# A two-stage transformer block on one core: the last FFN but one moved forward, VectorE steps moved by a slot, transposes released tile by tile

## The chip, the cores and the metric

The kernel runs on one core of one Trainium2 chip. TensorE (PE in the rows) multiplies and transposes, VectorE (DVE), ScalarE (ACT) and GpSimd (POOL) do the elementwise work, and SyncE's queue (SPq) issues the transfers. The metric is the device time of one execution in microseconds (us). The kernel before was timed three times and profiled once more.

## The reference

Sixteen sequences of 512 tokens with 256 features go through four residual steps. `a` is attention with 16 heads of 64, `b` is attention with 16 heads of 16 and rotary positions.

```python
x = x + attn_a(layernorm(x))      # returns X + gelu(A) @ Wpost, 16 heads of 64
x = x + ffn(layernorm(x))         # relu(x @ W1q.T + b1) @ W2q.T + b2, W1q and W2q of -1, 0, 1
x = x + attn_b(layernorm(x))      # rotary on q and k, 16 heads of 16, biases
x = x + ffn(layernorm(x))         # the same weights again
```

## The kernel before

The program is one list of slots per engine. Stage one (slots up to 540 or so) does attention `a` for all sequences and is not touched. Stage two starts 554 slots later (`SHIFT`) and does everything else. In stage two a slot is one unit of attention `b`: 32 units for each sequence, so that slots 32w to 32w+31 belong to sequence w. They are called **window w** here. A slot has two **steps**, and step r of window w is written r; slot k of a window holds steps 2k and 2k+1.

In each slot TensorE computes the scores of one unit (`scores`, L724), which VectorE reduces to their maximum (`unit_max`, L1160). From slot 11 of window 0 on, the scores of every unit go into the same PSUM banks, so the scores of slot k+1 wait for the maximum of slot k. TensorE then computes the turned scores of a unit 11 slots back (`turned_scores`, L738), which ScalarE exponentiates (`exps`, L867), and in every second slot the products with the values (`values`, L751). What TensorE does beside this is set by a table of steps for each sequence s, counted from step 64s. In steady state these fall into window w:

* first FFN of sequence w+2 ("ffn0"): transposes of the normalised tokens (`XT0`, steps 38 and 39 of the window), eight "up" products (`UP0`, steps 44 to 53), four "down" products (`DOWN0`, from step 56 on),
* q, k and v of sequence w+1 (`QK`, `VB`), their rotation on GpSimd (`ROTATE`), and the split into high and low parts: the high part on ScalarE (`parts_high`, L937, table `HIGHS`), the low part on VectorE (`parts_low`, L1154, table `LOWS`, steps 36, 38, 44 and 46 of the window),
* output projection ("wo", L767, `WO1`) and second FFN ("ffn1") of sequence w-1, whose `WO1` begins at step 34; the down products end in window w+1.

A layer norm is five VectorE or ScalarE pieces at the steps in `NORM`: statistics of two tiles (L1122), statistics of the other two, `aggregate` (L1128 to L1131), and twice two tiles normalised into the one buffer `xn` (L1136 on VectorE for ffn1, L875 on ScalarE for the others). The inverse deviation, a power over 4 columns, is GpSimd's (`inverse_deviation`, L554) and stands one step behind `aggregate` in GpSimd's own list. At the same place in that list stand the low parts of the hidden features (`hidden_low`, L569, three steps behind their "up"), and the addition of a bias to the four tiles at once (`add_bias`, L563, step 40 of the window for ffn0). After each transpose ScalarE makes the high part `xh` one step later and VectorE the low part `xl` two steps later (L1219). The high part of the first hidden tile (`hidden_high`, L919) waits until all low parts of the rotated q and k (L1154) are made, since they share memory. Every engine works through its list in order, and a wait holds back all that stands behind it.

Each engine's loop fixes the order inside one step. For VectorE it is:

```python
for todo in steps_of.get(step - 1, []): empty(*todo)
for todo in steps_of.get(step - 2, []): empty_low(*todo)
...
if step % 2 == 0 and 0 <= step // 2 < UNITS_ALL: unit_max(step // 2)
...
for piece, part, s in norm_steps.get(step, []): ...   # statistics, aggregate, normalise
... invert_sums, scale_heads, parts_low
```

For GpSimd `hidden_low` of step - 3 stands ahead of `inverse_deviation` of step - 1, and that ahead of `add_bias`.

The buffer `x_before` holds the tokens of one sequence from its output projection to the end of its second FFN. It is loaded at step 93 (`load_before`, L441), after the save of the sequence before (`save_before`, L446) has landed.

Of the kernel before, what the change touches and what calls it, by code (L numbers as in the profile page):

```python
# [13 lines left out]
def hybrid_block_kernel(nc, X, WQ, WK, WV, WPOST, WB, BQK, BV, WO, BO, W1T, B1, W2T, B2, COS, SIN, X1, M1, OUT):  # L14
# [6 lines left out]
    BATCH, S, D = X.shape  # L21
    TB = S // P
    KT = D // P
# [6 lines left out]
    FT = FF // P  # L30
# [9 lines left out]
    with ctx:  # L40
# [51 lines left out]
        wo = at("wo", 30, [P, QUADS // 2, D])  # L92
# [78 lines left out]
        xn_ready = sem("xn_ready")  # L171
# [65 lines left out]
        def bank(fill):  # L237
            return banks[fill % 3]
# [67 lines left out]
        QK, VB = (-41.5, -40, -38, -36), (-34, -33.5, -31.6, -31.1)  # L306
        WO1, XT1 = (98.5, 100.5, 104.5, 106.5), (118.1, 119.1)
        UP1, DOWN1 = (128, 129, 130.5, 132, 133, 134.5, 136.5, 138.5), (140.5, 142.5, 146.5, 148.5)
        NORM = {"ffn0": (-101, -100, -98, -93, -91), "attn": (-67, -64, -63, -51, -49), "ffn1": (103, 108, 109, 113, 115)}
        UP_RAMP, DOWN_RAMP, XTB_RAMP = tuple(range(-66, -58)), (-57, -55.5, -54, -52.5), (-45.9, -44.9)  # L310
        ATTN_RAMP = (-54, -51, -50, -48, -47)
        BIAS = {"ffn0": -88, "attn": -45, "ffn1": 124}
        ROTATE, HIGHS, LOWS = (-39, -37, -35, -34, -32, -30), (-31, -29, -23, -21), (-28, -26, -20, -18)
        STACK = (-17, -15, -11, -9, 5, 7, 21, 23)
        INVERT, SCALE_HEADS = (41, 57, 73, 90), (46, 62, 76, 92)
        SLOT = 2 * UNITS
# [2 lines left out]
        plan = []  # L319
        for s in range(BATCH):  # L320
            plan += [(XT0[k], "transpose", "ffn0", k, s) for k in range(KT)]
            plan += [((UP_RAMP if s == 1 else UP0)[f], "up", "ffn0", f, s) for f in range(FT)]
            plan += [((DOWN_RAMP if s == 1 else DOWN0)[t], "down", "ffn0", t, s) for t in range(TB)]
            plan += [((XTB_RAMP if s == 1 else XTB)[k], "transpose", "attn", k, s) for k in range(KT)]
            plan += [(QK[j], "qk", "attn", j, s) for j in range(4)]
            plan += [(VB[t], "v", "attn", t, s) for t in range(TB)]
            plan += [(WO1[t], "wo", "ffn1", t, s) for t in range(TB)]
            plan += [(XT1[k], "transpose", "ffn1", k, s) for k in range(KT)]
            plan += [(UP1[f], "up", "ffn1", f, s) for f in range(FT)]
            plan += [(DOWN1[t], "down", "ffn1", t, s) for t in range(TB)]  # L330
        plan = sorted((SLOT * s + at_step, kind, part, i, s) for at_step, kind, part, i, s in plan)

        at_of = {}
# [18 lines left out]
                    steps_of.setdefault(step, []).append((kind, part, i, s, fill))  # L352

        def norm_at(part, s):
            return ATTN_RAMP if (part, s) == ("attn", 1) else NORM[part]

        norms = sorted((SLOT * s + norm_at(part, s)[0], part, s) for s in range(BATCH) for part in NORM)
        nth_norm = {(part, s): n for n, (_, part, s) in enumerate(norms)}
# [31 lines left out]
        with nc.Block() as block:  # L390
            @block.sync
            def _(sp):
# [101 lines left out]
                for slot in range(FIRST_A, LAST + SHIFT):  # L494
# [15 lines left out]
                    for step in (2 * (slot - SHIFT), 2 * (slot - SHIFT) + 1):  # L510
                        for s in range(BATCH):
# [10 lines left out]
                                max_rows(s, (r - 12) // 8)  # L522
                            if r == 93:
                                load_before(s)
                            if r == 152:
                                save_before(s)
                sp.wait_ge(x_out, 16 * BATCH)

# [1 line left out]
            def _(pool):  # L530
# [64 lines left out]
                for slot in range(FIRST_A, LAST + SHIFT):  # L595
# [13 lines left out]
                    for step in (2 * (slot - SHIFT), 2 * (slot - SHIFT) + 1):  # L609
# [8 lines left out]
                        for s in range(BATCH):  # L618
                            r = step - SLOT * s
                            for part in NORM:  # L620
                                if r == BIAS[part]:
                                    add_bias(part, s)
                            if r in ROTATE and (s or r < ROTATE[3]):
                                rotate(ROTATE.index(r), s)

            @block.tensor
            def _(pe):
# [127 lines left out]
                def product(kind, part, i, s, fill):  # L755
# [10 lines left out]
                        for g in range(QUADS // 2):  # L766
                            last = mm(half, heads_b[:, g, tokens], wo[:, g, :], start=(g == 0), stop=(g == QUADS // 2 - 1))  # L767
                    elif kind == "transpose":
                        pe.wait_ge(xn_ready, TB * (nth_norm[part, s] + 1))
                        for t in range(TB):  # L770
                            last = nc.tensor.transpose(bank(fill)[:, t * P:(t + 1) * P], xn[:, t, i * P:(i + 1) * P], ident[:, :])
                    elif kind == "up":
                        if part == "ffn0" and s == 0:
# [558 lines left out]
```

## Time and profile before

| | before |
|---|---|
| median of 3 runs | 3782.32 us |
| lowest and highest | 3780.09 and 3784.66 us |
| the profiled execution's own time | 3781.21 us |
| its span in the profile | 3779.0 us |
| busy: PE, DVE, ACT, POOL | 3626.6, 2584.8, 2385.9, 1888.6 us |
| granted TensorE clock over the span | 0.986 of full speed |

Stage two begins at about 2248 us of the span. A number in the rows such as `[1.09 <-DVE max_b L1160]` is idle time of the engine just before the instruction, and what ended it. Neighbouring instructions of an engine are pipelined, so that one may start shortly before the end of the last. All times in the rows are from the start of the span.

### The profile page before, as it was taken

The page shows a single profiled execution, that of the slowest core. Times are in us where ns is not written, and L with a number is a line of the kernel's source. Part 1 is how long each engine was busy: PE and PEld are TensorE (multiplying, and loading weights), DVE is VectorE, ACT ScalarE, POOL GpSimd, SP SyncE. Part 2 cuts the span into 40 slices and gives each one's busy share as a digit, 9 for nine tenths or more (in the row PEclk, how much of TensorE's full clock was granted, in tenths as well). Part 3 has the DMA queues.
Part 4 walks back from the last instruction along what each step waited for, and adds up shares of the span by engine and source line. Part 5 has one row for each costly group of instructions (what it writes and reads, how often), then busy time and mean ns, then how long its engine had stood idle before and what let it go on. Part 6 is the DMA issues. An engine that isn't in the chain of part 4 may idle for free.

```text
span 3779.0 us, 64440 instructions
## 1 busy us (share of the span) xinstructions
PE 3626.6 (96%) x23810; PEld 2433.1 (64%) x23810; DVE 2584.8 (68%) x4296; ACT 2385.9 (63%) x4629; POOL 1888.6 (50%) x1337
## 2 busy tenths in 40 slices
PE   8999999999999999999999978999999999999987
PEld 6777777777777777777777664555555555555534
DVE  6766666666667666666767656777777777777763
ACT  5665656556566566655656546777777777777754
POOL 4555555556555555555654633444444444444412
PEclk9999999999999999999999998999999999999989
DMA  2000000000000000000000012222222222222220
GB/s 79 7 12 1 12 12 12 1 12 12 1 12 12 1 12 12 9 5 12 12 1 15 25 43 47 53 62 62 63 62 61 61 63 58 62 59 64 53 48 18
DMA packets 102329, 116.27 MB, mean 31 GB/s; under 512 B 23557, under 2 KB 75269, under 8 KB 102021
## 3 DMA queue, kind: packets, MB, share of 16 engines
q1 hardware_dynamic: 102020, 112.17, 12.0%
q8 instruction: 193, 3.16, 0.4%
q14 instruction: 116, 0.94, 0.1%
HBM read 34.48 MB, written 27.26 MB: 16 GB/s over the span
## 4 chain that ended last, share of the span: by engine, by line
PE 76%; DVE 11%; ACT 7%; issue 5%; POOL 1%; DMA 0%; DVEq 0%; ACTq 0%; SPq 0%
PE ps_o L675 12%; PE ps_s L644 10%; PE ps_t L657 8%; PE ps_t L226 8%; PE ps_m L657 4%; PE ps_o L751 4%; PE ps_t L233 4%; DVE max_b L1160 4%; PE ps_t L786 4%; PE ps_m L226 3%; PE ps_t L710 3%; PE ps_s L724 3%; ACT et L867 2%; PE ps_m L233 2%; PE ps_s L738 2%
## 5 line engine op out<-in xcount | busy, mean ns | idle before, releaser
L534 POOL TENSOR_TENSOR e_a<-e_a,recip 128x1024 f32<-128x1024 f32 x512 | 969.4, 1894 | 948.7 <-DVE recip L1027 948.5
L825 ACT ACTIVATE e_a<-ps_s,neg_max 128x512 f32<-128x512 f32 x1024 | 695.1, 685 | 544.8 <-DVE neg_max L1020 544.4
L1160 DVE TENSOR_REDUCE max_b<-ps_s 128x2 f32<-128x1024 f32 x512 | 625.0, 1221 | 270.6 <-PE ps_s L724 268.8
L867 ACT ACTIVATE et<-ps_s 128x1024 f32<-128x1024 f32 x512 | 527.4, 1030 | 319.9 <-PE ps_s L738 319.0
L1020 DVE TENSOR_REDUCE neg_max<-ps_s 128x2 f32<-128x1024 f32 x512 | 623.0, 1217 | 67.7 <-PE ps_s L644 67.7
L675 PE MATMUL ps_o<-et_a,v_a 128*64 128x256 f32 x4096 | 499.8, 386 | 9.1 <-DVE heads_a L1063 4.8
L644 PE MATMUL ps_s<-raw_a 64*128 64x512 f32 x3072 | 425.9, 409 | 5.5 <-ACT e_a L825 5.3
L675 PEld LDWEIGHTS ps_o<-et_a,v_a 128*64 128x64 f32 x4096 | 279.2, 137 | 192.1 <-issue 78.3
L657 PE MATMUL ps_t<-ident,e_a 128*128 128x128 f32 x2660 | 394.0, 280 | 2.1 <-DVE xl L1219 2.0
L1034 DVE COPY et_a<-ps_t 128x512 f32<-128x512 f32 x366 | 251.1, 688 | 206.3 <-PE ps_t L657 202.1
L657 PEld LDWEIGHTS ps_t<-ident,e_a 128*128 128x128 f32 x2660 | 290.1, 141 | 133.2 <-issue 129.3
L569 POOL TENSOR_TENSOR h_lo<-h,h_hi 128x512 fp32r<-128x512 f32 x215 | 276.1, 1290 | 179.6 <-ACT h_hi L919 177.5
L644 PEld LDWEIGHTS ps_s<-raw_a 64*128 64x128 f32 x3072 | 270.2, 184 | 129.2 <-issue 74.2
L724 PE MATMUL ps_s<-k_stack,q_stack 48*128 48x512 f32 x1024 | 261.0, 506 | 64.1 <-DVE max_b L1160 61.4
L751 PE MATMUL ps_o<-et,v_b 128*32 128x512 f32 x2048 | 283.0, 625 | 0.0
L573 POOL TENSOR_TENSOR m_parts<-max_b,m_parts 128x8 fp32r<-128x8 f32 x128 | 28.2, 221 | 481.6 <-ACT m_parts L909 481.6
L832 ACT ACTIVATE et_a<-ps_t 128x512 f32<-128x512 f32 x299 | 178.4, 597 | 115.7 <-PE ps_t L657 115.7
L724 PEld LDWEIGHTS ps_s<-k_stack,q_stack 48*128 48x128 f32 x1024 | 97.7, 186 | 233.2 <-DVE max_b L1160 107.8
L738 PE MATMUL ps_s<-q_stack,k_stack 50*128 50x512 f32 x1024 | 214.0, 412 | 11.1 <-ACT et L867 10.4
L657 PE MATMUL ps_m<-ident,e_a 128*128 128x128 f32 x1436 | 224.6, 279 | 0.0
L1045 DVE SCALAR_TENSOR_TENSOR raw_a<-ps_t,raw_a 128x512 fp32r<-128x512 f32 x181 | 124.3, 687 | 129.9 <-ACT raw_a L851 124.8
L825 ACT ACTIVATION_READ_ACCUMULATOR e_a<-ps_s,neg_max 128x1 f32 x1024 | 202.8, 198 | 0.0
(194 smaller groups left out, 7231.0 us busy)
## 6 DMA issues: line engine op xcount, KB each, us to landing
q_stack<-roped_q SPq DMA_DIRECT2D x256, 96.0 KB
k_stack<-roped_k SPq DMA_DIRECT2D x256, 96.0 KB
x_a<-X SPq DMA_DIRECT2D x16, 512.0 KB, 3.4
X<-x_a SPq DMA_DIRECT2D x16, 512.0 KB, 2.9
x_ahead<-X SPq DMA_DIRECT2D x16, 512.0 KB, 3.8
X<-x_ahead SPq DMA_DIRECT2D x16, 512.0 KB, 2.9
x_before<-X SPq DMA_DIRECT2D x16, 512.0 KB, 3.9
OUT<-x_before SPq DMA_DIRECT2D x16, 512.0 KB, 5.2
```

Source lines behind the costliest of these rows:

```text
L226: last = nc.tensor.matmul(out, w[:, k, c0:c0 + P], xs[:, k, :], start=(i == 0), stop=(i == len(todo) - 1))
L534: nc.gpsimd.tensor_tensor(e_a[:, u % 5, :, :], e_a[:, u % 5, :, :], factor, ALU.mult).then_inc(e_normed, 1)
L644: last = mm(ps_s[:, 2 * j + h, :], raw[rows, q_part, c:c + P], raw[rows, k_part, :], start=(m == 0), stop=(m == 2))
L657: last = nc.tensor.transpose(bank(fill)[:, c:c + P], e_a[:, u % 5, j, t * P:(t + 1) * P], ident[:, :])
L675: last = mm(out, v_a[:, t, c:c + HA], et_a[:, 2 * (q % 2):2 * (q % 2) + 2, t, h, :], start=(t == 0), stop=(t == TB - 1))
L724: last = mm(ps_s[:, score_bank(u) + h, :], q_stack[rows, pair, block_ * P:(block_ + 1) * P], k_stack[rows, pair, :], start=True, stop=True)
L738: last = mm(ps_s[:, 2 + h, :], k_stack[rows, pair, keys * P:(keys + 1) * P], q_stack[rows, pair, :], start=True, stop=True)
L751: last = mm(ps_o[32 * h:32 * (h + 1), :], v_b[:, s % 2, keys, 4 * quad + h, :], et[:, (2 * w + h // 2) % 5, h % 2, :], start=(keys == 0), ...
L825: ins = nc.scalar.activation(e_a[:, u % 5, h, :], ps_s[:, 2 * (u % 2) + h, :], ACT.Exp, bias=neg_max[:, u % 5, h:h + 1], accum_out=sums[:, ...
L867: nc.scalar.activation(et[:, v % 5, :, :], ps_s[:, 2:4, :], ACT.Exp)\
L1020: nc.vector.reduce_max(neg_max[:, u % 5, :], ps_s[:, 2 * (u % 2):2 * (u % 2) + 2, :], AX.X, negate=True)\
L1160: nc.vector.reduce_max(max_b[:, u // 4 % 2, :, u % 4], ps_s[:, score_bank(u):score_bank(u) + 2, :], AX.X, negate=True).then_inc(max_done, 1)
```

## The change

Four parts.

1. For sequence 14 alone, the output projection, the transposes, the up and the down products, the norm, the bias and the save get earlier steps (`WO_EARLY` and so on): wo from step 34.5 of window 15 to 31.5, the up products from 64 to 46.1, the down products from 76.5 to 57.5 and the save from 88 to 66. Slots 21 to 31 of the last window have neither ffn0 nor q, k and v products, since no sequences follow.
2. In every window the second low part of q moves from step 38 to 40 (`LOWS`).
3. For every other sequence the ffn1 statistics move from steps 39 and 44 of the window to 43 and 45, and `aggregate` from 45 to 46.
4. In stage two the first transposes of a norm wait for their token tiles one by one and not for all four.

```diff
-        NORM = {..., "ffn1": (103, 108, 109, 113, 115)}
+        NORM = {..., "ffn1": (107, 109, 110, 113, 115)}
+        WO_EARLY, XT_EARLY, FFN_EARLY = (95.5, 96.5, 98.5, 99.5), (107.1, 108.1), (99, 101, 102, 104, 105)
+        UP_EARLY, DOWN_EARLY = (110.1, 111, 112, 113.5, 115, 116.5, 118, 119), (121.5, 123.5, 125.5, 127)
+        BIAS_EARLY, SAVE_EARLY = 107, 130
...
-        ROTATE, HIGHS, LOWS = (-39, -37, -35, -34, -32, -30), (-31, -29, -23, -21), (-28, -26, -20, -18)
+        ROTATE, HIGHS, LOWS = (-39, -37, -35, -34, -32, -30), (-31, -29, -23, -21), (-28, -24, -20, -18)
...
-            plan += [(WO1[t], "wo", "ffn1", t, s) for t in range(TB)]
-            plan += [(XT1[k], "transpose", "ffn1", k, s) for k in range(KT)]
-            plan += [(UP1[f], "up", "ffn1", f, s) for f in range(FT)]
-            plan += [(DOWN1[t], "down", "ffn1", t, s) for t in range(TB)]
+            early = s == BATCH - 2
+            plan += [((WO_EARLY if early else WO1)[t], "wo", "ffn1", t, s) for t in range(TB)]
+            plan += [((XT_EARLY if early else XT1)[k], "transpose", "ffn1", k, s) for k in range(KT)]
+            plan += [((UP_EARLY if early else UP1)[f], "up", "ffn1", f, s) for f in range(FT)]
+            plan += [((DOWN_EARLY if early else DOWN1)[t], "down", "ffn1", t, s) for t in range(TB)]
...
+            return FFN_EARLY if (part, s) == ("ffn1", BATCH - 2) else NORM[part]
...
-                            if r == 152:
+                            if r == (SAVE_EARLY if s == BATCH - 2 else 152):
                                 save_before(s)
...
-                                if r == BIAS[part]:
+                                if r == (BIAS_EARLY if (part, s) == ("ffn1", BATCH - 2) else BIAS[part]):
                                     add_bias(part, s)
...
                     elif kind == "transpose":
-                        pe.wait_ge(xn_ready, TB * (nth_norm[part, s] + 1))
                         for t in range(TB):
+                            if i == 0:
+                                pe.wait_ge(xn_ready, TB * nth_norm[part, s] + t + 1)
                             last = nc.tensor.transpose(...)
```

**VectorE, window 10, slots 19 to 21.** This is the piece from the maximum of slot 19 to that of slot 21, first before. `roped_q` is the low part of q, `token_rows` and `recip_b` are the inversion of the softmax sums.

```order
L1160 TENSOR_REDUCE max_b<-ps_s 128x2
L1154 TENSOR_TENSOR roped_q<-q_rot,roped_q 128x512
L1122 BN_STATS stats<-x_before 128x6 x2
L1219 TENSOR_TENSOR xl<-ps_t,xh 128x512
L1160 TENSOR_REDUCE max_b<-ps_s 128x2
L1219 TENSOR_TENSOR xl<-ps_m,xh 128x512
L1199 STREAM_TRANSPOSE token_rows<-weighted 128x512
L1201 RECIPROCAL recip_b<-token_rows 128x16
L1160 TENSOR_REDUCE max_b<-ps_s 128x2
```

The same piece in the changed kernel:

```order
L1167 TENSOR_REDUCE max_b<-ps_s 128x2
L1226 TENSOR_TENSOR xl<-ps_t,xh 128x512
L1167 TENSOR_REDUCE max_b<-ps_s 128x2
L1161 TENSOR_TENSOR roped_q<-q_rot,roped_q 128x512
L1226 TENSOR_TENSOR xl<-ps_m,xh 128x512
L1206 STREAM_TRANSPOSE token_rows<-weighted 128x512
L1208 RECIPROCAL recip_b<-token_rows 128x16
L1167 TENSOR_REDUCE max_b<-ps_s 128x2
```

The low part has moved from ahead of the maximum of slot 20 to behind it, and the statistics have left the piece; they come behind the maximum of slot 21.

**GpSimd, a window of the steady state, from the ffn0 bias on.** `rstd` is the power, `h_lo` the low parts of the hidden tiles. Before:

```order
L573 TENSOR_TENSOR m_parts<-max_b,m_parts 128x8
L563 TENSOR_TENSOR x_ahead<-x_ahead,b_rows 128x1024
L554 TENSOR_TENSOR rstd<-rstd,minus_half 128x4
L569 TENSOR_TENSOR h_lo<-h_107,h_hi 128x512 x2
L573 TENSOR_TENSOR m_parts<-max_b,m_parts 128x8
L569 TENSOR_TENSOR h_lo<-h_107,h_hi 128x512 x5
```

In the changed kernel:

```order
L569 TENSOR_TENSOR x_ahead<-x_ahead,b_rows 128x1024
L575 TENSOR_TENSOR h_lo<-h_107,h_hi 128x512
L560 TENSOR_TENSOR rstd<-rstd,minus_half 128x4
L575 TENSOR_TENSOR h_lo<-h_107,h_hi 128x512
L579 TENSOR_TENSOR m_parts<-max_b,m_parts 128x8
L575 TENSOR_TENSOR h_lo<-h_107,h_hi 128x512 x5
```

The power now stands behind the first low part of the hidden tiles. This is so in windows 1 to 13, where a ffn1 norm and the up products of ffn0 meet.

**TensorE, window 15, slots 23 to 25.** Before, the three slots hold the attention's own products alone:

```order
L724 MATMUL ps_s<-k_stack,q_stack 128x512 x2
L738 MATMUL ps_s<-q_stack,k_stack 128x512 x2
L751 MATMUL ps_o<-et,v_b 32x512 x4
L724 MATMUL ps_s<-k_stack,q_stack 128x512 x2
L738 MATMUL ps_s<-q_stack,k_stack 128x512 x2
```

In the changed kernel, the same place up to the scores of slot 24:

```order
L730 MATMUL ps_s<-k_stack,q_stack 128x512 x2
L744 MATMUL ps_s<-q_stack,k_stack 128x512 x2
L757 MATMUL ps_o<-et,v_b 32x512 x4
L784 MATMUL ps_t<-xh,w_80 128x512 x2
L784 MATMUL ps_t<-xl,w_80 128x512 x2
L784 MATMUL ps_m<-xh,w_80 128x512 x2
L784 MATMUL ps_m<-xl,w_80 128x512 x2
L730 MATMUL ps_s<-k_stack,q_stack 128x512 x2
```

Two up products of sequence 14 have come between the values of slot 23 and the scores of slot 24.

## Rows read from the trace of the kernel before

**Rows 1.** Waits of TensorE over the whole span: total us, times, longest.

```profile
PE ps_s L724 <- DVE max_b L1160: 61.4, 90, 1.5
...
PE ps_m L771 <- ACT xn L875: 10.1, 2, 6.4
```

**Rows 2.** Timeline of VectorE: the maximum of slot 19 in windows 8 and 9.

```profile
3035.56 1.21 DVE L1160 TENSOR_REDUCE max_b<-ps_s 128x2 f32<-128x1024 f32 x1
...
3127.96 1.21 DVE L1160 TENSOR_REDUCE max_b<-ps_s 128x2 f32<-128x1024 f32 x1
```

**Rows 3.** Timeline of VectorE in window 10, slots 18 to 25 (start, us).

```profile
3220.17 1.21 DVE L1154 TENSOR_TENSOR roped_q<-q_rot,roped_q 128x512 fp32r<-128x512 f32 x1
...
3221.90 1.21 DVE L1160 TENSOR_REDUCE max_b<-ps_s 128x2 f32<-128x1024 f32 x1
...
3224.30 0.67 DVE L1219 TENSOR_TENSOR xl<-ps_t,xh 128x512 fp32r<-128x512 f32 x1
3224.89 1.21 DVE L1160 TENSOR_REDUCE max_b<-ps_s 128x2 f32<-128x1024 f32 x1
3226.02 0.68 DVE L1219 TENSOR_TENSOR xl<-ps_m,xh 128x512 fp32r<-128x512 f32 x1
...
3227.64 1.23 DVE L1160 TENSOR_REDUCE max_b<-ps_s 128x2 f32<-128x1024 f32 x1
...
3234.06 0.69 DVE L1154 TENSOR_TENSOR roped_k<-k_rot,roped_k 128x512 fp32r<-128x512 f32 x1
...
3236.09 2.21 DVE L1136 TENSOR_SCALAR xn<-x_before,mean_var,rstd 128x256 f32<-128x256 f32 x2
3238.22 1.21 DVE L1160 TENSOR_REDUCE max_b<-ps_s 128x2 f32<-128x1024 f32 x1
```

**Rows 4.** Timeline of TensorE in window 10: the scores of slots 21, 22 and 26.

```profile
3226.15 0.50 PE L724 MATMUL ps_s<-k_stack,q_stack 48*128 48x512 f32 x2 [1.09 <-DVE max_b L1160]
...
3228.92 0.50 PE L724 MATMUL ps_s<-k_stack,q_stack 48*128 48x512 f32 x2
...
3240.19 0.50 PE L724 MATMUL ps_s<-k_stack,q_stack 48*128 48x512 f32 x2
```

**Rows 5.** Timeline of GpSimd in window 10, slots 17 to 25.

```profile
3218.32 2.51 POOL L587 TENSOR_TENSOR k_rot<-k_rot 128x512 f32<-128x512 f32 x2
...
3224.58 2.37 POOL L563 TENSOR_TENSOR x_ahead<-x_ahead,b_rows 128x1024 f32<-128x1024 f32 x1
3232.77 1.02 POOL L554 TENSOR_TENSOR rstd<-rstd,minus_half 128x4 f32<-128x4 f32 x1 [5.83 <-DVE rstd L1131]
3235.55 2.59 POOL L569 TENSOR_TENSOR h_lo<-h,h_hi 128x512 fp32r<-128x512 f32 x2 [1.77 <-ACT h_hi L919]
```

**Rows 6.** Timeline of ScalarE in window 10: the first hidden tile's high part.

```profile
3234.84 0.63 ACT L919 ACTIVATE h_hi<-h 128x512 fp32r<-128x512 f32 x1 [1.43 <-DVE roped_k L1154]
```

**Rows 7.** Timeline of VectorE in window 15: the maximum of slots 0 and 11.

```profile
3625.04 1.23 DVE L1160 TENSOR_REDUCE max_b<-ps_s 128x2 f32<-128x1024 f32 x1 [0.72 <-PE ps_s L724]
...
3658.70 1.22 DVE L1160 TENSOR_REDUCE max_b<-ps_s 128x2 f32<-128x1024 f32 x1
```

**Rows 8.** Timeline of TensorE: the first two output projections of the last sequence.

```profile
3739.68 3.42 PE L767 MATMUL ps_m<-wo,heads_b 128*128 128x256 f32 x8 [3.05 <-DVE heads_b L1213]
```

**Rows 9.** Timeline of SyncE's queue: the load of sequence 14's `x_before`.

```profile
3670.09 0.38 SPq L441 DMA_DIRECT2D x_before<-X  x1
```

**Rows 10.** Timeline of ScalarE: exponentials of turned scores behind the last scores.

```profile
3704.35 1.02 ACT L867 ACTIVATE et<-ps_s 128x1024 f32<-128x1024 f32 x1 [0.65 <-PE ps_s L738]
...
3705.97 1.03 ACT L867 ACTIVATE et<-ps_s 128x1024 f32<-128x1024 f32 x1 [0.39 <-PE ps_s L738]
...
3733.57 1.03 ACT L867 ACTIVATE et<-ps_s 128x1024 f32<-128x1024 f32 x1 [2.50 <-PE ps_s L738]
```

**Rows 11.** Timeline of VectorE: residual of the last output projection.

```profile
3744.57 0.69 DVE L1186 TENSOR_TENSOR x_before<-x_before,ps_m 128x512 f32<-128x512 f32 x1 [5.04 <-DMA x_before<-X]
```

**Rows 12.** Busy time in a stretch of window 15: PE, PEld, DVE, ACT, POOL, granted clock.

```profile
3668.00:3675.00 7.00, 5.87 (x20) 2.35 (x20) 2.67 (x4) 2.26 (x3) 0.20 (x1) 0.52 0.31 87
```

More of the change, by code:

```diff
@@ L308, in hybrid_block_kernel @@
         UP1, DOWN1 = (128, 129, 130.5, 132, 133, 134.5, 136.5, 138.5), (140.5, 142.5, 146.5, 148.5)
-        NORM = {"ffn0": (-101, -100, -98, -93, -91), "attn": (-67, -64, -63, -51, -49), "ffn1": (103, 108, 109, 113, 115)}
+        NORM = {"ffn0": (-101, -100, -98, -93, -91), "attn": (-67, -64, -63, -51, -49), "ffn1": (107, 109, 110, 113, 115)}
+        WO_EARLY, XT_EARLY, FFN_EARLY = (95.5, 96.5, 98.5, 99.5), (107.1, 108.1), (99, 101, 102, 104, 105)
+        UP_EARLY, DOWN_EARLY = (110.1, 111, 112, 113.5, 115, 116.5, 118, 119), (121.5, 123.5, 125.5, 127)
+        BIAS_EARLY, SAVE_EARLY = 107, 130
         UP_RAMP, DOWN_RAMP, XTB_RAMP = tuple(range(-66, -58)), (-57, -55.5, -54, -52.5), (-45.9, -44.9)
@@ L354, in norm_at @@
         def norm_at(part, s):
-            return ATTN_RAMP if (part, s) == ("attn", 1) else NORM[part]
+            if (part, s) == ("attn", 1):
+                return ATTN_RAMP
+            return FFN_EARLY if (part, s) == ("ffn1", BATCH - 2) else NORM[part]
         norms = sorted((SLOT * s + norm_at(part, s)[0], part, s) for s in range(BATCH) for part in NORM)
```

## Prediction

> **What bounds the kernel now.** I read the table of busy time first, then TensorE's waits, then the timeline of one window of the steady state, and the end last. TensorE is busy for 3626.6 of 3779.0 us, so what counts is any time in which it waits, and any wait that is added. Its largest wait is for the running maximum on VectorE: 61.4 us in 90 places [rows 1]. The windows repeat: the maximum of slot 19 comes 92.40 us after that of the window before (3035.56 to 3127.96), and 93.94 us in the next one (3221.90) [rows 2, 3]. The second figure matters: in that window something held the engines up for 1.5 us, and the windows after it run 1.5 us later. A delay of TensorE inside a window is carried to the end in full, and the same holds for a gain. I take window 10 as the pattern.
>
> There the scores of slot 21 wait 1.09 us for the maximum of slot 20 [rows 4]. VectorE was late with it: between the maxima of slots 19 and 20 (3221.90 and 3224.89) stand the second low part of q, the statistics and `xl` [rows 3]. The change takes the first two out of this place. That is its gain, and it can be at most 1.09 us in a window.
>
> **Parts 2 and 3, where the moved instructions come to stand (windows 1 to 13).** Step by step, in the times of window 10:
>
> (a) Between the two maxima only `xl` is left. It began at 3224.30 behind the others and now begins when ScalarE's part is there, at about 3223.3, so the maximum of slot 20 starts near 3224.0 instead of 3224.89 and ends near 3225.2. The scores of slot 21 come 0.9 us earlier.
>
> (b) The low part of q now starts at 3225.2. GpSimd is then in its bias addition, from 3224.58 to 3226.95 [rows 5]. What that does is seen one slot earlier in the same trace: the first low part of q starts at 3220.17 while GpSimd works until 3220.83 (3218.32 + 2.51) and takes 1.21 us, ending 0.55 us after GpSimd, where a low part without such a neighbour takes 0.69 [rows 3, 5]. `xl`, which reads PSUM, takes 0.68 beside the bias addition, undisturbed [rows 3, 5]. So the low part ends at 3226.95 + 0.55 = 3227.5. Behind it stand `xl`, the transposition and the reciprocal, 1.62 us as before (3226.02 to 3227.64) [rows 3]. The maximum of slot 21 starts at 3229.0 instead of 3227.64, and the scores of slot 22 at 3230.3 instead of 3228.92 [rows 4]: the gain has become a loss of 1.4 us.
>
> The Trainium skill says of this place (SBUF — State Buffer, section Who interferes with whom) that a VectorE instruction with two SBUF inputs and a GpSimd instruction that reads SBUF exclude each other for the whole of the one that came first. By that rule as written the low part would run its full 0.69 us after GpSimd and not 0.55, and 13 windows would cost 1.8 us more than the sum below.
>
> (c) The statistics and `aggregate` now stand in slots 21 to 23, so VectorE is behind with each maximum. Adding the spacings of its instructions, the maximum of slot 22 starts at 3231.8, of slot 23 at 3234.3, and the last low part of k, in slot 23, ends at 3237.0 instead of 3234.75 (3234.06 + 0.69) [rows 3]. ScalarE's high part of the first hidden tile waits for just that: it starts at 3237.1 instead of 3234.84 [rows 6].
>
> (d) GpSimd now makes the low part of that tile before the power. It can start at 3237.8 (0.71 us behind the high part, as in rows 5 and 6), takes 1.3 us, and the power 1.02 [rows 5]: the inverse deviation is there at 3240.1, where before it was there at 3233.8. VectorE's `xn` stands behind the maximum of slot 24, which ends at 3238.2, and waits for it with the maximum of slot 25 queued behind. The two tiles of `xn` took 2.21 us beside GpSimd's low parts [rows 3, 5]; between 1.7 (one GpSimd instruction in the way) and 3.0 us (two) are possible now. The maximum of slot 25 then starts between 3241.8 and 3243.1 instead of 3238.22, and the scores of slot 26 between 3243.1 and 3244.4 instead of 3240.19 [rows 3, 4]. That is 2.9 to 4.2 us a window. I take 3.5, near the middle, because nothing tells which of the two it will be. Slots 26 to 31 are bound by TensorE and hide nothing.
>
> Thirteen windows: 13 x 3.5 = +45.5 us (37.7 to 54.6). Window 0 has (b) without statistics: +1 (0 to 1.4). Window 14 has no bias addition and no ffn0 products: 0.
>
> **Part 1, the last window.** The slots without added products are set by VectorE: the maximum, then 0.6 us until the next scores are there, about 1.9 us a slot. Slots 0 to 10 of the window, with the same up and down products of sequence 13, took 33.66 us for 11 slots [rows 7]. The early FFN puts these products into slots 23 to 31, nine slots. I take off the one empty slot (1.8 us) and the attention of another (1.2), and get 30.7 us. The transfer into `x_before` is issued at 3670.09 [rows 9] and lands about 4 us later, but the first residual now stands in VectorE's list at slot 16, about 3670; VectorE waits there until 3674, and the norm's pieces fall into VectorE-bound slots, so slot 23 begins some 2.3 us later than before. Slot 31 then ends near 3718.5. Behind it eleven turned scores are left, at 1.62 us each, as between 3704.35 and 3705.97, where before they took 27.6 us for ten beside the FFN [rows 10]. The last exponential starts at 3735 by this and 3733.57 before [rows 10]; with TensorE at half clock for part of it, as it fell after sparse slots in the granted clock of 0.52 from 3668 to 3675 [rows 12], 3735 to 3739. Then two gains: no down product of sequence 14 stands ahead of the last values (-0.9), and the last residual, which waited 5.04 us for its transfer until 3744.57 [rows 11], waits for its own products only (-1.3, as they end at 3743.1 [rows 8]). Together +1 us, between -1.5 and +4. So what the change was to remove from behind the last scores comes back in front of them, almost to the microsecond.
>
> **Part 4.** The last token tile arrives when it did, and only three transposes move ahead of it, some 0.5 us at each place where TensorE waits for `xn`: two at the ramp, where it waits 10.1 us in all [rows 1], and one at the end. -1.5 us (0 to -2). In the steady state TensorE doesn't wait there: 0.
>
> **Sum.** +45.5 + 1 + 1 - 1.5 = +46 us against the profiled execution's 3781.2, so 3827.2; the median of the runs is 1.1 above it: 3828 us. Its own range, from the bounds, is 3814 to 3843.
>
> **The rivals.**
>
> *Half of it: GpSimd does not hold the low part up.* Then (b) costs nothing, slot 22 is 0.3 us early, but (d) remains, since it hangs on the order in GpSimd's list: the power at 3238.4, the scores of slot 26 at 3242.0, +1.8 us a window, 13 x 1.8 = 23, so 3805 us. Against it speaks the 1.21 us of the first low part; for it that no row shows this very pair. 0.17.
>
> *Faster.* The bias addition and the reversed order fall into idle time, and the wait at slot 21 disappears: 13 x 1.09 = -14, and -1 at the ends: 3767 us. It needs the power done before the maximum of slot 24 has ended (3238.2), that is, a first hidden tile whose high part starts by 3235.2, as it did before (3234.84). With VectorE late by (c) it does not. 0.07.
>
> *No change.* The gain at slot 21 and the later waits cancel because ScalarE, relieved by the delay, catches up for the rest of the window: 3782 us. The 1.5 us that were carried on in full speak against it. 0.05.
>
> *The last window costs much more.* As forecast, and the dense slots 23 to 31 are bound by ScalarE (an exponential and two hidden-tile instructions for each up product), then the turned scores run at half clock throughout: +11 instead of +1, 3838 us. 0.09.
>
> **How the numbers follow.** The forecast has 0.62. A measurement of this kernel can tell about 0.2% from no change, 7.6 us. Faster is the one rival, 0.07; same is no change, 0.05; slower is the rest, 0.88. The range takes in the forecast's own, the last rival and most of the first: 3795 to 3845 us.
>
> **What the changed profile would show.** TensorE's wait of 1.09 us at slot 21 gone or small, and new ones at slots 22 and 26, released by the maximum. The second low part of q at 2.3 us instead of 0.7, ending half a microsecond behind the bias addition. On VectorE an idle time before `xn`, released by the power, in 13 windows. The distance of the windows 95 to 96.5 us instead of 92.4. No wait for the transfer at the end, and one for it near slot 16 of window 15. I would be wrong if the distance stays at 92.4 or falls: then (c) and (d) hide, and the step to look at is the time of the power. If the distance is right and the sum is not, the last window is mis-sized.

## The result, and the profile after

The changed kernel takes 3830.91 us (median of four runs, 3825.96 to 3833.61) and the kernel before, in four runs beside it, 3783.49: a ratio of 1.0124 (95% interval 1.0106 to 1.0141), slower by 47.4 us. The profiled execution has a span of 3830.2 us. The busy times of the engines, two groups of VectorE's, and four of TensorE's waits (total us, times, longest):

```profile
PE 3651.6 (95%) x23810; PEld 2443.5 (64%) x23810; DVE 2618.1 (68%) x4296; ACT 2387.1 (62%) x4629; POOL 1893.0 (49%) x1337
```

```profile
L1161 DVE TENSOR_TENSOR roped_q<-q_rot,roped_q 128x512 fp32r<-128x512 f32 x32 | 54.6, 1708 | 0.0
...
L1143 DVE TENSOR_SCALAR xn<-x_before,mean_var,rstd 128x256 f32<-128x256 f32 x64 | 51.1, 841 | 24.7 <-POOL rstd L560 24.7
```

```profile
PE ps_s L730 <- DVE max_b L1167: 80.8, 87, 2.8
...
PE ps_s L744 <- ACT et L874: 16.0, 27, 1.2
...
PE ps_m L778 <- ACT xn L882: 7.1, 2, 5.0
...
PE ps_t L778 <- DVE xn L1143: 4.5, 1, 4.5
```

The second fence gives, per group, busy time and mean of one in ns. The 32 low parts of q take 54.6 us instead of 29.4, and the longest wait for a maximum is 2.8 us where it was 1.5 [rows 1]. VectorE waits 24.7 us for the power, in front of `xn`.

**Where the time arose.** The two profiled spans differ by 51.2 us. I measured a window by the distance of its maximum of slot 19 to the next one's. It was 92.40 us [rows 2]. Of windows 2 to 13, four now have 94.4 (window 13, whose successor has fewer products, 93.83 where it had 91.80), five have 95.1 to 95.6 and three 96.6 to 96.7. Window 4 begins and ends with these rows of VectorE:

```profile
2677.21 1.21 DVE L1167 TENSOR_REDUCE max_b<-ps_s 128x2 f32<-128x1024 f32 x1
...
2772.77 1.21 DVE L1167 TENSOR_REDUCE max_b<-ps_s 128x2 f32<-128x1024 f32 x1
```

The first maximum of window 15 was at 3625.04 [rows 7] and is at 3666.30, 41.3 us later. Counted from the first maximum of a window to that of the next, 38.5 us of it come from windows 1 to 13, 2.3 from window 0 and 0.5 from before and behind them. The last window and the end add 10 us.

**Window 3, the plain case.** VectorE, from the maximum of slot 19 to that of slot 25:

```profile
2582.84 1.21 DVE L1167 TENSOR_REDUCE max_b<-ps_s 128x2 f32<-128x1024 f32 x1
2584.20 0.69 DVE L1226 TENSOR_TENSOR xl<-ps_t,xh 128x512 fp32r<-128x512 f32 x1 [0.15 <-ACT xh L896]
2584.81 1.22 DVE L1167 TENSOR_REDUCE max_b<-ps_s 128x2 f32<-128x1024 f32 x1
2585.94 2.46 DVE L1161 TENSOR_TENSOR roped_q<-q_rot,roped_q 128x512 fp32r<-128x512 f32 x1
...
2589.94 1.23 DVE L1167 TENSOR_REDUCE max_b<-ps_s 128x2 f32<-128x1024 f32 x1
...
2596.83 0.68 DVE L1161 TENSOR_TENSOR roped_k<-k_rot,roped_k 128x512 fp32r<-128x512 f32 x1
...
2600.62 1.70 DVE L1143 TENSOR_SCALAR xn<-x_before,mean_var,rstd 128x256 f32<-128x256 f32 x2 [1.97 <-POOL rstd L560]
2602.24 1.21 DVE L1167 TENSOR_REDUCE max_b<-ps_s 128x2 f32<-128x1024 f32 x1
```

GpSimd in the same window:

```profile
2585.48 2.38 POOL L569 TENSOR_TENSOR x_ahead<-x_ahead,b_rows 128x1024 f32<-128x1024 f32 x1
2598.32 1.29 POOL L575 TENSOR_TENSOR h_lo<-h,h_hi 128x512 fp32r<-128x512 f32 x1 [10.46 <-ACT h_hi L926]
2599.57 1.02 POOL L560 TENSOR_TENSOR rstd<-rstd,minus_half 128x4 f32<-128x4 f32 x1
```

The second low part of q starts at 2585.94, inside GpSimd's bias addition, and ends at 2588.40, 0.54 us after the addition (2585.48 + 2.38 = 2587.86). Behind it the maximum of slot 21 is late. TensorE's four waits between slots 19 and 31 of this window are these:

```profile
2584.20 0.50 PE L730 MATMUL ps_s<-k_stack,q_stack 48*128 48x512 f32 x2 [0.22 <-DVE max_b L1167]
...
2591.22 0.50 PE L730 MATMUL ps_s<-k_stack,q_stack 48*128 48x512 f32 x2 [2.35 <-DVE max_b L1167]
...
2600.40 0.49 PE L744 MATMUL ps_s<-q_stack,k_stack 50*128 50x512 f32 x2 [0.45 <-ACT et L874]
...
2603.51 0.50 PE L730 MATMUL ps_s<-k_stack,q_stack 48*128 48x512 f32 x2 [0.49 <-DVE max_b L1167]
```

They sum to 3.51 us. Before, window 10 has three, for the scores of slots 20, 21 and 29:

```profile
3223.26 0.50 PE L724 MATMUL ps_s<-k_stack,q_stack 48*128 48x512 f32 x2 [0.19 <-DVE max_b L1160]
...
3248.92 0.50 PE L724 MATMUL ps_s<-k_stack,q_stack 48*128 48x512 f32 x2 [0.51 <-DVE max_b L1160]
```

With the 1.09 at slot 21 [rows 4] that is 1.79. The difference, 1.72, accounts for nearly all of the 1.97 by which the windows lie further apart. This bookkeeping (what TensorE waits, summed over a window) served for the experiments below, where it meets the distance within 0.3 us.

**Window 4, with the clock.** Here the same wait is followed by something that window 3 doesn't have:

```profile
2685.62 0.80 PE L730 MATMUL ps_s<-k_stack,q_stack 48*128 48x512 f32 x2 [2.37 <-DVE max_b L1167]
...
2686.77 1.22 PE L784 MATMUL ps_t<-xh,w 128*128 128x512 f32 x2
...
2691.47 0.73 PE L784 MATMUL ps_t<-xh,w 128*128 128x512 f32 x2
```

```profile
2681.20:2685.50 4.30, 2.05 (x12) 0.76 (x12) 4.23 (x6) 2.15 (x3) 1.05 (x1) 1.00 0.00 0
2685.60:2689.00 3.40, 3.38 (x9) 2.32 (x10) 3.40 (x8) 1.14 (x2) 0.00 (x0) 0.51 0.05 10
```

The columns of the second fence are the stretch, its length, the busy time of PE, PEld, DVE, ACT and POOL, the granted clock, and the share and rate of the DMA. From 2685.6 to 2689.0 TensorE is granted 0.51, its lower level of 1.2 GHz, after a stretch in which it was busy for 2.05 of 4.3 us. In window 3 it was busy for 2.07 us of the same stretch, and the clock did not fall. The up products that take 0.73 us at 2691.47 take 1.22 at 2686.77. Nine of windows 1 to 13 have such a stretch behind the wait at slot 22, and each costs 1.2 us (95.56 from 2677.21 to 2772.77, against 94.37 in window 3).

The kernel before has exactly one, in window 9, and it is the 1.5 us that the prediction had noticed and left at "something held the engines up". TensorE and the stretch, in the kernel before:

```profile
3132.21 0.60 PE L724 MATMUL ps_s<-k_stack,q_stack 48*128 48x512 f32 x2 [1.10 <-DVE max_b L1160]
...
3133.17 1.93 PE L751 MATMUL ps_o<-et,v_b 128*32 128x512 f32 x8
```

```profile
3132.50:3135.90 3.40, 3.40 (x14) 0.99 (x13) 2.47 (x5) 1.97 (x2) 0.47 (x1) 0.50 0.00 0
```

Eight value products take 1.93 us there, and 1.07 at full clock, behind a wait of 1.10 us for the maximum of slot 20.

### The profile page after: what moved, and what is told of

It is laid out like the page before. It is cut to its first block, busy times and chain, and to the rows that moved or that the text cites. A ratio compares the mean times of both kernels' runs of the same rounds, so it can differ in the third digit from the quotient of the medians.

```text
span 3830.2 us, 64392 instructions
## 1 busy us (share of the span) xinstructions
PE 3651.6 (95%) x23810; PEld 2443.5 (64%) x23810; DVE 2618.1 (68%) x4296; ACT 2387.1 (62%) x4629; POOL 1893.0 (49%) x1337
## 4 chain that ended last, share of the span: by engine, by line
PE 79%; DVE 10%; ACT 4%; issue 4%; POOL 1%; DMA 0%; SPq 0%; DVEq 0%; ACTq 0%
PE ps_o L681 12%; PE ps_s L650 10%; PE ps_t L663 8%; PE ps_t L226 8%; PE ps_o L757 5%; PE ps_m L663 4%; PE ps_t L793 4%; PE ps_s L730 4%; PE ps_t L233 4%; PE ps_m L226 3%; PE ps_t L716 3%; DVE max_b L1167 3%; PE ps_s L744 2%; PE ps_t L784 2%; PE ps_m L233 2%
```

## The experiments

I held that GpSimd's bias addition holds the low part up and that this is most of the loss; the rivals were the reversed order of the power and the first low hidden part, the later statistics as such, and the early FFN. Each of the four parts was first made alone on the kernel before; then single steps were put back in the changed kernel. "Distance" is that of the windows, from the profile.

**Part 2 alone.**

```diff
-        ROTATE, HIGHS, LOWS = (-39, -37, -35, -34, -32, -30), (-31, -29, -23, -21), (-28, -26, -20, -18)
+        ROTATE, HIGHS, LOWS = (-39, -37, -35, -34, -32, -30), (-31, -29, -23, -21), (-28, -24, -20, -18)
```

> The kernel before with part 2 alone: the second low part of q at step 40 instead of 38, the statistics where they were. Theory (the low part is held up by GpSimd's bias addition): it takes 2.3 to 2.5 us instead of 0.68, the scores of slot 22 come 1.4 us later, and the windows are 93.8 us apart instead of 92.4; 14 windows make about +20 us, 3803 us, more where the TensorE clock falls behind the new wait. Rival (the low part costs nothing at its new place, only the wait at slot 21 shrinks): windows 91.8 to 92.4 us apart, 3775 to 3783 us.

Measured: 3813.95 us against 3786.80, ratio 1.0074 (1.0057 to 1.0090). VectorE and GpSimd in window 5 of this kernel:

```profile
2776.23 2.05 DVE L1154 TENSOR_TENSOR roped_q<-q_rot,roped_q 128x512 fp32r<-128x512 f32 x1
```

```profile
2775.36 2.38 POOL L563 TENSOR_TENSOR x_ahead<-x_ahead,b_rows 128x1024 f32<-128x1024 f32 x1
```

The low part starts 0.41 us later behind the maximum of slot 19 than in the changed kernel, since the statistics still stand ahead of it, takes 2.05 us instead of 2.46 and ends at the same place, 0.54 us behind the addition. The distance is 93.6 in the four of windows 1 to 13 without a stretch at the lower clock and 94.7 to 94.9 in the nine that have one (94.18 in window 13). TensorE's waits in window 5 sum to 2.94, +1.15 against before; the distance is 1.17 longer. More than half of the whole loss is this one step on the list: 27 us, where 20 were expected, since 13 x 1.17 is 15 us and the stretches at the lower clock add some 11.

**Part 3 alone.**

```diff
-        NORM = {..., "ffn1": (103, 108, 109, 113, 115)}
+        NORM = {..., "ffn1": (107, 109, 110, 113, 115)}
```

> The kernel before with part 3 alone: ffn1 statistics and aggregate at steps 43, 45 and 46. Theory (the power behind the first low part of the hidden tiles in GpSimd's list holds up the normalisation and the maximum of slot 25): slot 22 0.5 us earlier, slot 26 1.0 to 2.3 us later, windows 93.4 to 94.7 us apart, 13 windows make +13 to +30 us, about 3803 us. Rival (only the low part costs): windows 91.9 us apart or less, 3775 us.

Measured: 3786.41 against 3786.80, ratio 1.0004 (0.9995 to 1.0013), distance 92.53, no stretch at the lower clock. The time is that of the kernel before, against an expected 3803 us. The power is late as forecast, and `xn` waits for it:

```profile
2778.87 1.69 DVE L1136 TENSOR_SCALAR xn<-x_before,mean_var,rstd 128x256 f32<-128x256 f32 x2 [1.97 <-POOL rstd L554]
```

```profile
2778.65 0.51 PE L738 MATMUL ps_s<-q_stack,k_stack 50*128 50x512 f32 x2 [0.63 <-ACT et L867]
...
2781.75 0.50 PE L724 MATMUL ps_s<-k_stack,q_stack 48*128 48x512 f32 x2 [0.47 <-DVE max_b L1160]
```

The maximum of slot 25 comes 17.57 us after that of slot 19 (2762.91 in this window) instead of 16.32 [rows 3], and that of slot 28 at 25.89 instead of 25.75. TensorE waits 1.77 us in the window, as before (1.79): 0.64 less at slot 21, nothing at slot 29, and 1.10 more at slots 25 and 26. VectorE's late maximum was paid for out of waits that were there anyway.

**Part 1 alone,** the `_EARLY` tables.

> The kernel before with part 1 alone: the second FFN of sequence 14 early. The profile of the changed kernel puts window 15 and what follows at +10 us, where the forecast had +1. Theory (part 1 costs this by itself): windows 0 to 14 as before, maxima of slots 0 to 31 of window 15 94 us apart instead of 79, the turned scores behind them at half clock, 3791 to 3794 us. Rival (the 10 us come from the other parts or from the late state in which window 15 begins): 3781 to 3785 us.

Measured: 3791.54 against 3786.80, ratio 1.0014 (1.0004 to 1.0023). Distances as before. From the first maximum of window 15 to the end it takes 160.7 us instead of 154.0, +6.7. In three pieces: first to last maximum 91.8 us instead of 79.1 (+12.7); last maximum to last exponential 24.2 instead of 29.5 (-5.3); from there to the end 44.7 instead of 45.4 (-0.8). So the second piece doesn't give back what the first costs. In it TensorE has only the turned scores. The stretch in this kernel:

```profile
3729.00:3750.00 21.00, 14.18 (x56) 3.00 (x54) 2.75 (x6) 9.39 (x10) 0.00 (x0) 0.53 0.08 25
```

It is busy for 14.18 of 21 us and granted 0.53. In the kernel before, the FFN of sequence 14 filled this place:

```profile
3704.00:3722.00 18.00, 16.66 (x87) 8.11 (x84) 3.75 (x7) 16.30 (x25) 8.93 (x8) 1.00 0.01 3
```

There TensorE was busy for 16.66 of 18 us, at full clock. The other profiles say the same. In all six kernels with part 1 (this one, the changed one and four further down) a stretch of 20 to 27 us at the lower clock begins behind the last scores; in the seven without it there is none longer than 4 us up to the last exponential.

**Part 4 alone.**

```diff
-                        pe.wait_ge(xn_ready, TB * (nth_norm[part, s] + 1))
                         for t in range(TB):
+                            if i == 0:
+                                pe.wait_ge(xn_ready, TB * nth_norm[part, s] + t + 1)
```

> The kernel before with part 4 alone: transposes released tile by tile. Theory: windows 1 to 14 unchanged at 92.4 us, TensorE's waits for the normalised tokens shorter by some 0.5 us at each of three places, -1.5 us in all, 3782 us, which the times can't tell from no change. Rival (single waits cost TensorE's queue time at each of the 48 transposes): windows longer by 0.2 us or more.

Measured: 3780.98 against 3786.80, ratio 0.9986 (0.9976 to 0.9995). The waits of TensorE for `xn`, 10.1 us [rows 1] and 5.7 before, are smaller:

```profile
PE ps_m L772 <- ACT xn L876: 7.1, 2, 5.0
...
PE ps_t L772 <- DVE xn L1137: 4.0, 1, 4.0
```

It is the one part of the change that shows a gain by itself.

**The power ahead of the low hidden part,** in the changed kernel.

```diff
+                        for piece, part, s in norm_steps.get(step - 1, []):
+                            if piece == 2:
+                                inverse_deviation(part, s)
...
-                        for piece, part, s in norm_steps.get(step - 1, []):
-                            if piece == 2:
-                                inverse_deviation(part, s)
```

> The changed kernel with GpSimd's list mended: the power stands ahead of the low parts of the hidden tiles again. Theory (low part held up by the bias addition costs most, the power's place adds 0.8 us a window): the low part still takes 2.46 us, windows without a fall of the clock 93.6 to 94.0 us apart instead of 94.4, with a fall 1.2 us more, in all 8 to 12 us less than the changed kernel, about 3821 us. Rival (the power's place is the main cost): windows 92.4 us apart, 3792 us.

Measured: 3829.72 against 3786.86, ratio 1.0103 (1.0088 to 1.0118). In window 4 of this kernel the power no longer stands behind a low hidden part, and `xn` doesn't wait:

```profile
2691.94 1.12 POOL L560 TENSOR_TENSOR rstd<-rstd,minus_half 128x4 f32<-128x4 f32 x1 [10.01 <-DVE rstd L1138]
```

```profile
2694.01 2.32 DVE L1143 TENSOR_SCALAR xn<-x_before,mean_var,rstd 128x256 f32<-128x256 f32 x2
```

Yet `xn` takes 2.32 us instead of 1.69 (two low hidden parts run beside it from 2693.59 on), and the distance falls by 0.14 us alone (94.23 without, 95.43 with a stretch at the lower clock), where at least 0.4 were expected. The three windows of 96.7 us are gone, but twelve of windows 1 to 13 have a stretch at the lower clock instead of nine, which takes most of that back: about 1 us less in all than the changed kernel, where 8 to 12 were expected. In a plain window, a step that VectorE waited 2 us for was worth next to nothing.

**The bias one step earlier,** in the changed kernel: GpSimd's addition then begins 0.4 us before the maximum of slot 19 and not 2.6 us behind it.

```diff
-        BIAS = {"ffn0": -88, "attn": -45, "ffn1": 124}
+        BIAS = {"ffn0": -89, "attn": -45, "ffn1": 124}
```

> The changed kernel with the ffn0 bias addition one step earlier in GpSimd's list, so that it starts about 3 us earlier and is over when the second low part of q comes. Theory: that low part takes 0.68 us again, the wait at slot 22 shrinks below 0.6 us, the clock doesn't fall in windows 2 to 13, windows 92.6 to 93.2 us apart, 3795 to 3800 us, of which 7 to 10 us are the early FFN's. Rival (the low part is long at its new place for another reason): 2.46 us and windows 94.4 to 96.7 us apart as in the changed kernel.

Measured: 3791.27 against 3786.86, ratio 1.0014 (1.0004 to 1.0023). Window 5:

```profile
2761.46 0.68 DVE L1161 TENSOR_TENSOR roped_q<-q_rot,roped_q 128x512 fp32r<-128x512 f32 x1
```

```profile
2757.89 2.37 POOL L569 TENSOR_TENSOR x_ahead<-x_ahead,b_rows 128x1024 f32<-128x1024 f32 x1 [0.65 <-ACT xn L882]
```

The addition ends at 2760.26, the low part starts at 2761.46 and takes 0.68. The distance is 92.6, no window has a stretch at the lower clock, and TensorE's waits sum to 1.70. One number in the table of biases takes away 43 of the 47 us, some 4 more than expected.

**Both.**

> The changed kernel with both mended, bias addition and power first. Theory: windows 92.1 to 92.4 us apart, the scores of slot 22 0.3 us earlier than before, and what is left is the early FFN: 3788 to 3792 us. Rival (statistics so late cost by themselves, since VectorE is behind from slot 21 to 24): windows 92.8 us or more.

Measured: 3787.09 against 3786.86, ratio 1.0000 (0.9990 to 1.0009); distance 92.45, just above the expected 92.1 to 92.4, and so not the 92.8 of the rival.

**Both, without part 1.**

> As the run with both mended, without the early FFN (parts 2, 3 and 4 with the bias addition and the power first). Theory: windows 92.1 to 92.4 us apart and the end of the kernel before, 3777 to 3783 us, the lowest time of all. Rival (as for the run with both mended): windows 92.8 us or more, 3787 us.

Measured: 3784.42 against 3786.86, ratio 0.9991 (0.9981 to 1.0000). The windows are as forecast, 92.45 us apart, but the time is not the lowest of all: 3777 to 3783 us were expected. The two medians differ by 2.7 us and their intervals overlap, so these runs don't show that the early FFN costs anything in this setting. The profiled execution, the slowest of the ten, takes 160.0 us from the first maximum of window 15 to the end, 6 more than the kernel before, although the FFN of sequence 14 is at its old place. The lower clock lies ahead of the last scores there:

```profile
3691.50:3715.20 23.70, 20.11 (x76) 7.23 (x75) 15.08 (x24) 10.75 (x14) 4.01 (x5) 0.50 0.02 3
```

The profile with part 2 alone has the same from 3715.5 to 3739.4. So the last window can be slow without part 1 too, and why it was in these two is open.

**The hold-up in the kernel before.** Only the bias moves, by one step; nothing of the change is made. The addition now lies on the low part's old place.

```diff
-        BIAS = {"ffn0": -88, "attn": -45, "ffn1": 124}
+        BIAS = {"ffn0": -89, "attn": -45, "ffn1": 124}
```

> The kernel before with one edit that the change does not have: the ffn0 bias addition one step earlier in GpSimd's list, so that it falls on the second low part of q at its old place. Theory (a VectorE instruction with two SBUF inputs waits for GpSimd's): that low part starts 1.13 us and the bias addition 0.4 us before to the maximum of slot 19, runs until 0.55 us behind the end of the addition and takes 1.3 us instead of 0.68; the maximum of slot 20 comes 0.6 us later and the windows are 93.0 us apart, 3788 to 3792 us. Rival (the long low part is a matter of its place in VectorE's list): 0.68 us and 92.4 us.

Measured: 3810.88 against 3784.86, ratio 1.0075 (1.0062 to 1.0087).

```profile
2768.43 2.38 POOL L563 TENSOR_TENSOR x_ahead<-x_ahead,b_rows 128x1024 f32<-128x1024 f32 x1 [0.62 <-ACT xn L875]
```

```profile
2770.01 1.33 DVE L1154 TENSOR_TENSOR roped_q<-q_rot,roped_q 128x512 fp32r<-128x512 f32 x1
```

The addition ends at 2770.81, the low part at 2771.34, 0.53 us behind it. Held up by 0.65 us, it makes the maximum of slot 20 late by 0.66 (3.65 us behind that of slot 19, before 2.99). The distance is 93.07 in the plain windows, +0.67, and 93.9 to 97.0 in the nine with stretches at the lower clock. The hold-up is as forecast and makes 9 of the 26 us; the time, 20 us above the forecast, is not, for the lower clock was left out of it. The same edit that mends the changed kernel spoils the one before.

**The changed kernel without part 2.**

> The changed kernel with part 2 alone undone (the second low part of q back at step 38). Theory (part 2 is what costs, through the hold-up by GpSimd, and brings the falls of the clock with it): windows 92.5 us apart, no fall of the clock in windows 2 to 13, and of the loss only the early FFN's 5 to 8 us left: 3788 to 3792 us. Rival (the four parts cost only together, or the late statistics do): 3805 us or more.

Measured: 3791.53 against 3784.86, ratio 1.0017 (1.0008 to 1.0026), distance 92.52, no stretch at the lower clock. So part 2 costs most of it and part 3 hardly anything without it. Together they cost more than apart, 1.97 us in a plain window against 1.17 and 0.13. The low part ends with GpSimd's addition in either case, so the maximum of slot 21 starts 7.10 us behind that of slot 19, with part 3 or without it. This is the maximum of slot 21 in window 5 with part 2 alone, where that of slot 19 starts at 2772.72:

```profile
2779.82 1.23 DVE L1160 TENSOR_REDUCE max_b<-ps_s 128x2 f32<-128x1024 f32 x1
```

What part 3 saves at slot 21 is lost in that hold-up, and the waits at slots 25 and 26 that it brings come on top.

**A milder early FFN with part 4, on the kernel before.** The up products begin at slot 26 of the last window, the first ones two slots apart, and the down products stay behind the last scores.

```diff
+        WO_EARLY, XT_EARLY, FFN_EARLY = (98.5, 100.5, 102.5, 104.5), (111.1, 112.1), (103, 105, 106, 108, 110)
+        UP_EARLY, DOWN_EARLY = (116, 120, 124, 128, 129, 130.5, 132.5, 134.5), (136.5, 138.5, 140.5, 142.5)
+        BIAS_EARLY, SAVE_EARLY = 121, 146
```

> The kernel before with part 4, and a milder early FFN for sequence 14: three up products in slots 26, 28 and 30 of the last window, which have no products with the values and so a wait of TensorE of about 1 us each, the rest behind the scores, down products and save three slots earlier than before. Theory (dense slots cost what they save, free ones don't): the last 31 maxima 79 to 81 us apart, turned scores behind them 3 to 4 us shorter, no wait for the transfer at the end, -3 to -6 us in all, 3776 to 3780 us. Rival (the clock takes it back: sparser turned scores at half clock): within 2 us of the kernel before.

Measured: 3779.87 against 3784.86, ratio 0.9991 (0.9982 to 1.0000). From the first maximum of window 15 to the end it takes 150.7 us, before 154.0 and with part 4 alone 151.4, and TensorE stays at full clock behind the last scores:

```profile
3708.00:3726.00 18.00, 16.01 (x94) 9.25 (x90) 3.10 (x8) 12.89 (x20) 6.57 (x6) 1.00 0.01 2
```

So spreading the FFN avoids the loss, but the gain over part 4 alone, 0.6 us in the profiles, is below what the runs can tell. Part 4 by itself is the best that I can name.

## Why the prediction was right, and where it was not

The forecast was 3828 us, and 3831 was measured. The mechanism was right for the first half of the window; the sum came out because wrong terms cancelled: the 13 windows' waits were priced 20 us too high (45.5 for 25.6), stretches at the lower clock and a late `xn` in three windows, 14 us, were not in the sum, and the last window was 9 us too low. The range from its own bounds was also added up wrongly at the lower end: the terms give 3816 to 3842, not 3814 to 3843.

**Step (a), right.** `xl` alone stands between the maxima, and the second of them starts 1.97 us after the first; the forecast had 2.1 (3224.0 against 3221.90). TensorE's wait at slot 21 is gone.

**Step (b), right.** In times after the maximum of slot 19, forecast and then measured: low part's end 5.6 and 5.56, maximum of slot 21 7.1 and 7.10, scores of slot 22 8.4 and 8.38. The bias one step earlier took all of it away, and the same hold-up appeared in the kernel before when the addition was moved onto its low part, so the cause is shown by runs in both directions. The Trainium skill (SBUF — State Buffer, Who interferes with whom) says that the pair of ports that the two share is an exclusive lock, and that the one that comes second blocks fully. The pairing that it names, a VectorE instruction with two SBUF inputs against GpSimd's, is the one seen. That the blocked one then needs its whole time doesn't hold here: it ends 0.53 to 0.54 us after GpSimd in three kernels, and alone it takes 0.68.

**Step (c), right within 0.4 us.** The maximum of slot 22 starts at 9.60 (forecast 9.9), that of slot 23 at 11.98 (12.4), and the first hidden tile's low part at 15.48 (15.9).

**Step (d), the one that failed.** "The maximum of slot 25 then starts between 3241.8 and 3243.1", that is 19.9 to 21.2 after slot 19; it was 19.40. `xn` took 1.69 us, my lower bound, where I had taken the middle. More important is the next sentence, "Slots 26 to 31 are bound by TensorE and hide nothing". The scores of slot 26 come at 20.67 instead of 18.29, +2.38 and not +3.5, and 0.4 of that is gone by slot 29, where TensorE had waited 0.51 us for a maximum before and no longer does. I had that row within reach and did not look past slot 26. So of the 3.5 us, 0.65 were `xn`, 0.4 the lateness carried over from (c), and 0.4 what slot 29 gives back. Of the 2.38 us at slot 26, 1.36 were there at slot 22 already (8.38 instead of 7.02), by (b) alone. The two runs on this step agree: late statistics alone cost 0.13 us a window, since the waits that go at slots 21 and 29 pay for the late maximum of slot 25, and the order of the power is worth 0.14. In the plain windows the loss is 1.97 us, not 3.5. The rival "half of it", 1.8 us a window, named almost this price, but for the opposite reason: it kept (d) and dropped (b), and the runs keep (b) and all but drop (d).

**What was not forecast.** TensorE's clock falls in nine of thirteen windows after the wait at slot 22, 1.2 us each, 11 us together. Three windows have a further 1.1 us, at slot 26, where the second pair of `xn` runs beside GpSimd longer:

```profile
2985.74 2.77 DVE L1143 TENSOR_SCALAR xn<-x_before,mean_var,rstd 128x256 f32<-128x256 f32 x2
```

It takes 2.77 us there and 1.67 us in window 10. With the power first none of the thirteen windows has this. So 13 x 1.97 + 9 x 1.2 + 3 x 1.1 = 39.7 us. The kernel before has one stretch of 1.5 us itself, which leaves 38.2; measured 38.5, forecast 45.5. That it comes so near to the forecast is luck. Window 0 cost 2.3 instead of 1, but executions of equal code differ by up to 3 us in windows 0 and 1, so nothing can be read from it.

**The last window, mis-sized.** "Together +1 us, between -1.5 and +4"; it was +10, against +6.7 with part 1 alone. The wait for the transfer is there as forecast, once, with 3.26 us:

```profile
3714.98 0.69 DVE L1193 TENSOR_TENSOR x_before<-x_before,ps_t 128x512 f32<-128x512 f32 x1 [3.26 <-DMA x_before<-X]
```

Of the three pieces, the first (to the last maximum) was forecast at about +13 us (3718.5 less the maximum's own 1.2, against 3704.12) and came to +12.7 with part 1 alone, +15.3 in the whole change, where slot 29 is at the lower clock. What failed is "Behind it eleven turned scores are left, at 1.62 us each" and the 2 us allowed for half clock "for part of it". The second piece took 25.1 us (24.2 with part 1 alone) where I had some 18 to 22. In the changed kernel, the maxima of slots 29 and 30, and two stretches:

```profile
3751.43 1.23 DVE L1167 TENSOR_REDUCE max_b<-ps_s 128x2 f32<-128x1024 f32 x1 [1.33 <-PE ps_s L730]
...
3758.10 1.22 DVE L1167 TENSOR_REDUCE max_b<-ps_s 128x2 f32<-128x1024 f32 x1
```

```profile
3750.00:3757.00 7.00, 6.96 (x31) 4.39 (x30) 1.44 (x3) 1.02 (x1) 0.00 (x0) 0.54 0.03 6
...
3767.50:3790.00 22.50, 15.54 (x58) 3.33 (x56) 1.96 (x4) 10.41 (x11) 0.00 (x0) 0.50 0.07 24
```

Slot 29 takes 6.67 us at a granted clock of 0.54 (4.01 in the kernel with part 1 alone), and from 3767.5 on the turned scores run at 0.50. Their exponentials come 1.92 and 2.58 us apart by turns instead of 1.62. The rival "the last window costs much more" had +11 by this very half clock, and it was what happened; I gave it 0.09. The rows for it were there: with sparse slots the clock was 0.52 [rows 12], and a tail of turned scores alone is sparse too.

**Part 4, right in sign.** Forecast -1.5 us. TensorE waits 3.0 us less for ScalarE's `xn` and 1.7 less for VectorE's with part 4 alone; the median is 5.8 lower, with an interval of 2 to 9 us. So the gain is shown and its size is not.

The rivals "faster" and "no change" fall: windows became longer by 2 to 4 us in every one of 1 to 13.

## What to carry to other kernels

Before a VectorE instruction with two SBUF inputs is moved by a slot, look at what GpSimd does at the new place; here one step on either list decided over 26 to 43 us in 3784. Price a delay by what the bounding engine will wait, summed to the end of the repeating piece, and not by how late the other engine becomes, for waits that are already there pay for part of it. Work that is taken from a sparse tail to fill earlier slots also takes away what kept TensorE's clock up in that tail.

## What I had not expected of the hardware

One wait of 2.35 us in a stream that is otherwise 97% busy was followed by 3.4 us at 1.2 GHz in nine windows of thirteen, and not in the other four, with the same instructions and the same wait (2.35 and 2.37 us). With the power first the same wait was followed by it twelve times of thirteen, with part 2 alone a wait of 1.95 us nine times, and with the bias moved in the kernel before one of 1.75 us nine times, for 3.4 to 10.2 us. The 1.10 us at slot 21 were followed by it once in thirteen windows in the kernel before, once each with part 1 and part 4 alone, and never in the kernel with the milder FFN. The Trainium skill (TensorE: Matmul & The Clock Gate, section A second HAM failure mode: psum-queue depth-cycling) tells of short idles between groups of matmuls that make the clock swing; these windows agree with it, though here it is one wait in a window. In the five kernels with the low part free and part 3 in (part 3 alone, the bias earlier, both, both without part 1, part 2 undone), where the longest wait here is 0.7 us, no window had it. So the falls go with the size of the wait. What decides between the nine and the four is open, and no run was made on it.
